# Overlapping two batch rows by two attention units, a tanh gate, and fewer TensorE passes in three small steps

## The reference

```
xn = layernorm(x)
# branch 1: attention with 16 heads of 8, causal
pressure = q k^T / sqrt(8), masked to -10000 above the diagonal
attn = 1 - tanh((pressure - threshold) / tau)^2, divided by its sum + 1e-6
s = (attn v) Wo^T
# branch 2: transformer block on xn
h = rmsnorm(xn); X = xn + softmax(q k^T / sqrt(8)) v wo      # not causal, 16 heads
h2 = rmsnorm(X); combine = weights of the 2 best of 8 experts, by token
moe = swiglu_shared(h2) + sum_e combine[e] * swiglu_e(h2)     # d_ff 256
g = silu(X + moe)
out = x + s * g
```

## Time and profile before

| what | value |
|---|---|
| median of three runs | 1170.88 us (1170.34 to 1171.27) |
| the profiled execution | 1171.43 us, span 1169.6 us |
| busy PE, DVE, ACT, POOL | 1055.8, 839.3, 648.9, 340.6 us |
| mean granted TensorE clock | 0.953 |
| from one gate to the next (first two) | 137.1 and 138.8 us |

### The profile page before, as it was taken

One profiled execution on the slowest core, in us unless ns is written; L12 is line 12 of the kernel. 1 busy time (PEld: TensorE's weight loads), 2 busy tenths in 40 slices (PEclk: granted clock), 3 DMA queues, 4 the chain that ended last, 5 costly groups with the idle time before them and its releaser, 6 DMA issues.

```text
span 1169.6 us, 18848 instructions
## 1 busy us (share of the span) xinstructions
PE 1055.8 (90%) x7112; PEld 487.0 (42%) x7112; DVE 839.3 (72%) x1692; ACT 648.9 (55%) x873; POOL 340.6 (29%) x178
## 2 busy tenths in 40 slices
PE   3469999899999899999999999989999999999998
PEld 1112465224651356424553246523464235532465
DVE  7366887659767687677876598765976868764872
ACT  4038842597227972388524983269722786248822
POOL 6500354005430335203351045301542033510023
PEclk9559999999998999999998999999999999989999
DMA  5530244104420045202350034400442012610020
GB/s 176 108 59 2 63 117 70 29 2 88 126 37 28 22 76 130 52 2 50 83 118 28 3 73 111 66 28 3 95 122 41 21 40 58 143 29 1 2 73 10
DMA packets 71787, 69.68 MB, mean 60 GB/s; under 512 B 8528, under 2 KB 63056, under 8 KB 71568
## 3 DMA queue, kind: packets, MB, share of 16 engines
q1 hardware_dynamic: 68928, 64.41, 25.0%
q10 hardware_dynamic: 2768, 4.06, 1.0%
HBM read 53.37 MB, written 14.81 MB: 58 GB/s over the span
## 4 chain that ended last, share of the span: by engine, by line
PE 66%; ACT 13%; DVE 12%; issue 4%; DMA 2%; SPq 2%; POOL 1%; ACTq 0%; POOLq 0%; DVEq 0%
PE O L977 12%; PE O L993 10%; ACT PT L534 7%; PE S L1009 6%; DVE PT L685 6%; PE M L919 6%; PE S L1011 6%; PE S L1010 6%; PE S L952 6%; PE M L916 5%; DVE nmax L648 3%; PE M L902 2%; ACT L534 2%; PE M L1082 2%; PE M L908 1%
## 5 line engine op out<-in xcount | busy, mean ns | idle before, releaser
L534 ACT ACTIVATE PT<-S 128x1024 f32<-128x1024 f32 (+1 forms) x448 | 420.0, 972 | 100.7 <-PE S L952 98.9
L648 DVE TENSOR_REDUCE nmax<-M 128x1 f32<-128x512 f32 x512 | 332.8, 685 | 121.1 <-PE M L916 75.5
L685 DVE SCALAR_TENSOR_TENSOR PT<-PT 128x768 f32<-128x768 f32 (+1 forms) x192 | 215.6, 1170 | 95.6 <-ACT PT L534 95.2
L977 PE MATMUL O<-PT,V 128*12 128x256 f32 (+3 forms) x2816 | 251.1, 438 | 0.0
L409 POOL TENSOR_TENSOR split<-split,parts 128x512 f32<-128x512 f32 x32 | 91.1, 2846 | 463.3 <-ACT parts L495 463.3
L952 PE MATMUL S<-stackQ,stackK 64*128 64x512 bf16 (+3 forms) x1024 | 202.1, 356 | 21.3 <-DMA stackQ<-mTZ 7.3
L568 ACT ACTIVATE PT<-S 128x1024 f32<-128x1024 f32 x72 | 73.9, 1027 | 257.9 <-PE S L1011 257.8
L424 POOL TENSOR_TENSOR PT<-PT,CB 128x1024 f32<-128x1024 f32 x56 | 133.3, 2387 | 283.7 <-DMA CB<-scrC 175.0
L1009 PE MATMUL S<-h2hi,wgu_hi 128*128 128x512 f32 x288 | 151.4, 526 | 0.0
L993 PE MATMUL O<-PT,wdn 128*128 128x512 f32 x288 | 142.8, 595 | 0.0
L916 PE MATMUL M<-KX,stackQ 128*128 128x512 bf16 x256 | 105.6, 414 | 26.0 <-DMA KX<-scrK 22.8
(11 more groups left out here) (177 smaller groups left out, 1034.8 us busy)
## 6 DMA issues: line engine op xcount, KB each, us to landing
CB<-scrC SPq DMA_DIRECT2D x64, 256.0 KB, 5.4
stackQ<-scrQ SPq DMA_DIRECT2D x192, 64.0 KB
stackK<-scrK SPq DMA_DIRECT2D x192, 64.0 KB
scrQ<-parts SPq DMA_DIRECT2D x16, 384.0 KB, 4.5
scrK<-parts SPq DMA_DIRECT2D x16, 384.0 KB, 8.7
KX<-scrK SPq DMA_DIRECT2D x96, 32.0 KB
PT<-in_w_gu ACTq DMA_DIRECT2D x2, 1152.0 KB, 7.8
xin<-in_x SPq DMA_DIRECT2D x8, 256.0 KB, 3.0
```

The costliest lines, as they stand in the source:

```text
L534: a.activation(PT[:, n % SLOTS, 2 * q * w:2 * q * w + 2 * w].rearrange("p (r n) -> p r n", r=2), S[k][:, :].rearrange("p (r n) -> p r n", ...
L648: v.tensor_reduce(nmax[:, h % 2, h // 2, t:t + 1], M[k][:, :], AX.X, ALU.max, negate=True).then_inc(m_read[k], 1)
L685: v.scalar_tensor_tensor(p, p, 1.0, p, ALU.subtract, ALU.mult).then_inc(weighed, 1)
L977: last = t_.matmul(O[k][32 * q:32 * q + VW, i0:i1], V[:, j, 4 * g + q, :], PT[:, n % SLOTS, w * q + at:w * q + at + i1 - i0], start=(j == ...
```

## The change

- **Rows overlap by two units.** The scores of units 0 and 1 of the next batch row, their exponentials, and the first maximum of run Y stand between the down products of experts 6, 7 and 8 of the present one. The gate goes into the next row: DVE takes part of it (`out_by_s`) in unit 0, ACT a tanh behind the exponentials of unit 1, DVE the rest (`out_gated`) in unit 1, and `outT` and its addition ride in unit 3. The store moves behind the load of `xin` on SP. Only the last row has its gate at its own end (`outL`).
- **The gate by tanh.** Silu(o) times s becomes (1 + tanh(o/2)) times (o times s/2): three operations instead of two.
- **Run X is cut in two**, X (pairs 0, 1) and W (pairs 2, 3), each with its own transpose, copy and four transfers. Unit 0 needs X alone, unit 4 needs W.
- **Fewer passes.** The masks of a unit with two key blocks are one matmul of 256 columns instead of two of 128. `suffix` uses sums of V that POOL makes (`VS`): 7 matmuls instead of 10. `combT` is a transpose instead of a product with the identity.

The core of the diff:

```diff
-RUNS = {"X": (0, 4), "Y": (4, 6), "Z": (6, 8)}
+RUNS = {"X": (0, 2), "W": (2, 4), "Y": (4, 6), "Z": (6, 8)}
...
-spread(MAX["Y"], {0: 1, 1: 4, 2: 4, 3: 4, 4: 3})
-spread(MAX["Z"], {4: 1, 5: 3, 6: 4, 7: 4, 8: 4})
+spread(MAX["Y"], {0: 1, 1: 3, 2: 4, 3: 4, 4: 4})
+spread(MAX["Z"], {5: 3, 6: 4, 7: 4, 8: 5})
+PLACES[3].insert(2, "outT")
...
-spread(MAX["X"], {EXPERT + e: n for e, n in enumerate((0, 0, 5, 4, 4, 5, 6, 6, 2))})
+spread(MAX["X"], {EXPERT + e: n for e, n in enumerate((0, 0, 5, 4, 4, 3))})
+spread(MAX["W"], {EXPERT + 5 + e: n for e, n in enumerate((2, 6, 6, 2))})
...
-PLACES[END - 1] += ["maxT_X"]
-PLACES[END] += ["outT"]
+PLACES[EXPERT + 6].insert(2, "maxT_X")
+PLACES[END] += ["maxT_W", "outL"]
...
+                g.tensor_tensor(VS[:, 1, :, :], V1[:, 2, :, 0:HD], V1[:, 3, :, 0:HD], ALU.add).then_inc(v_summed, 1)
+                wait_apart(pool, v_summed, it * 2 + 1)
+                g.tensor_tensor(VS[:, 0, :, :], V1[:, 1, :, 0:HD], VS[:, 1, :, :], ALU.add).then_inc(v_summed, 1)
...
-                act.wait_ge(down_done, it * DOWNS + DOWNS + DEPTH)
-                a.activation(gT[:, :], O[0][:, :], ACT.Silu).then_inc(o_read[0], 1)
+                if following:
+                    a.activation(warm[:, :], n1s[:, :], ACT.Exp)
+                    for q in range(2):
+                        weights(it + 1, 0, q)
+                    take(u, "maxT_W", bt)
+                    for q in range(2):
+                        weights(it + 1, 1, q)
+                act.wait_ge(out_scaled, it + 1)
+                a.activation(gT[:, :], O[0][:, :], ACT.Tanh, scale=0.5).then_inc(o_read[0], 1)
...
+            def out_by_s(it):
+
+                dve.wait_ge(down_done, (it + 1) * DOWNS + DEPTH)
+                dve.wait_ge(*read(ROWS[it], "proj1"))
+                v.tensor_tensor(sT[:, :], sT[:, :], O[0][:, :], ALU.mult).then_inc(out_scaled, 1)
+
+            def out_gated(it):
+
+                dve.wait_ge(o_read[0], (it + 1) * O_USES[0] + 1)
+                v.scalar_tensor_tensor(gT[:, :], gT[:, :], 1.0, sT[:, :], ALU.add, ALU.mult).then_inc(prod_ready, 1)
...
+                    if n == 0 and it > 0:
+                        out_by_s(it - 1)
+                    if n == 1 and it > 0:
+                        out_gated(it - 1)
...
+                        mask = never[:, :].unsqueeze(1).broadcast_to([128, len(js), 128])
...
-                        for j in range(t, NT):
-                            last = t_.matmul(M[k][:, t * 128:t * 128 + 128], (below if j == t else ones)[:, :],
-                                             V1[:, j, :, 0:HD], start=(j == t), stop=(j == NT - 1))
+                        last = t_.matmul(M[k][:, t * 128:t * 128 + 128], below[:, :], V1[:, t, :, 0:HD], start=True, stop=(t == NT - 1))
+                        if t < NT - 1:
+                            rest = V1[:, t + 1, :, 0:HD] if t == NT - 2 else VS[:, t, :, :]
+                            last = t_.matmul(M[k][:, t * 128:t * 128 + 128], ones[:, :], rest, start=False, stop=True)
...
-                        last = t_.matmul(M[k][0:E, t * 128:t * 128 + 128], comb[:, t, :], ident[:, :], start=True, stop=True)
+                        last = t_.transpose(M[k][0:E, t * 128:t * 128 + 128], comb[:, t, :], ident[:, :])
...
+                if following:
+                    first_scores(it + 1)
                 for _step in second_product(it, NE - 2):
                     pass
+                if following:
+                    work(u, it, "maxT_W")
+                    for q in range(2):
+                        scores(it + 1, 1, q)
+                    for name in ROWS[it + 1].places[0]:
+                        work(ROWS[it + 1], it + 1, name)
```

More of the change, by code:

```diff
@@ L119 @@
 FIRST = Uses(False, True)
-LOOP = Uses(True, True, FIRST.total)
-LAST = Uses(True, False, LOOP.row(B - 1).before)
+ROW0 = Uses(True, True, FIRST.total, behind=False)
+LOOP = Uses(True, True, tuple(f + r for f, r in zip(FIRST.total, ROW0.total)))
+ROWS = [ROW0] + [LOOP.row(it - 1) for it in range(1, B - 1)] + [Uses(True, False, LOOP.row(B - 2).before)]
 S_USES = UNITS + NE
@@ L369, in row @@
                     spread_weights(u, it)
-                wait_apart(sp, *read(u, "outT"))
-                sp.dma_start(out_t[bass.ds(it, 1)].rearrange("o p t d -> (o p) t d"), xres[:, :, :]).then_inc(written, 16)
-                wait_apart(sp, written, it * 16 + 16)
+                    store(u, it, "outL")
             sp.wait_ge(kset, 3)
             prepare(FIRST, 0)
-            for it in range(B - 1):
-                row(LOOP.row(it), it, True)
-            row(LAST, B - 1, False)
+            for it in range(B):
+                row(ROWS[it], it, it < B - 1)
         @block.gpsimd
@@ L601, in _ @@
             v = nc.vector
-            steps = [0, 0]
+            steps = [0]
             def step(ins, apart=False):
@@ L806, in row @@
                                 CB[:, E - 1, :].unsqueeze(1).broadcast_to([128, NFH, L]), ALU.mult).then_inc(routed_last, 1)
-                dve.wait_ge(o_read[0], it * O_USES[0] + O_USES[0] + 1)
-                dve.wait_ge(*read(u, "proj1"))
-                v.tensor_tensor(gT[:, :], gT[:, :], sT[:, :], ALU.mult).then_inc(prod_ready, 1)
-                k, _n = u("outT")
-                dve.wait_ge(*full(u, "outT"))
-                dve.wait_ge(xres_in, it * 16 + 16)
-                v.tensor_tensor(xres[:, :, :].rearrange("p t d -> p (t d)"), M[k][:, :],
-                                xres[:, :, :].rearrange("p t d -> p (t d)"), ALU.add).then_inc(m_read[k], 1)
-                assert steps[0] <= DVE_ROW and (not following or steps[0] == DVE_ROW), steps
+                if not following:
+                    out_by_s(it)
+                    out_gated(it)
+                    take(u, it + 1, "outL")
             for k in range(2):
@@ L1158, in _ @@
             first_scores(0)
-            for it in range(B - 1):
-                row(LOOP.row(it), it, True)
-            row(LAST, B - 1, False)
+            for q in range(2):
+                scores(0, 1, q)
+            for name in ROWS[0].places[0]:
+                work(ROWS[0], 0, name)
+            for it in range(B):
+                row(ROWS[it], it, it < B - 1)
 _INS = ["x", "par", "n1w", "n2w", "w1", "w2", "router", "w_gu", "w_dn"]
```

124 lines of the change are left out of this document (71 added, 53 removed).

## The result

| | median | runs |
|---|---|---|
| before | 1170.61 us | 4 (1169.96 to 1171.27) |
| after | 1155.16 us | 4 (1154.38 to 1157.05) |

The ratio is 0.988 [0.986, 0.990]: the change gains 15 us where 39 were forecast. 1155 lies outside the range of 1121 to 1152. The profiled execution took 1157.05 us with a span of 1155.2, the slowest of the four.

What follows compares the result with a forecast made beforehand. PE was taken to bound the experts, with PE, ACT and DVE waiting in turn at row ends. Terms -26.6 - 9.6 - 0.8 - 3.3 + 0.7 + 0.8 = -38.8 us from 1171.4 gave 1132; range 1121 to 1152.

Steps and rivals of the forecast that it cites:

- What bounds the kernel, and D to Z: Experts bound by PE; from D, a row's last down product, to run Z's split 23.8 us instead of 27.8.
- rivals (a) to (d): Behind D: clock still falls 1144 (0.18); DVE keeps waits 1149 (0.14); DVE back-to-back 1117 (0.10); no boundary gain 1160 (0.05).
- The rule of the Trainium skill on transposes and the clock gate: Transposes don't count as busy for the clock, so outT's four in unit 3 could help bring on a fall: 1144.
- One sign of being wrong: Listed signs: PE waits in the tail for S1 or W's split, at outT, or longer for Z's rows at unit 12.
- the prediction's 0.25: Behind D, each us at half clock was priced at 0.25 us of added time.
- A boundary gains 3.8 us: At each batch row's end the overlap saves 3.8 us; seven boundaries give -26.6 us.
- D at 349.3: 0.2 us later: Row's tail on PE: 7.6 us from 341.7, so the last down product ends its wait 0.2 us later, without new waits.
- Run X in two: in the shade of the experts' PE work but for the transpose, +0.7: In the experts: one more transpose and DVE split per row, hidden but for the transpose; +0.7 us in all.
- First row: -3.3: Kernel start: unit 0's wait for transfers hidden under W's maxima, 4.2 us less 0.9 for a second run.
- Suffix, combT, masks: Fewer PE passes: suffix and combT 1.2 us per row, -9.6 for eight; masks 0.1 per row, -0.8.
- The last gate: End of the last row: three gate operations in a chain instead of two, +0.8 us.
- the five rivals: Four alternatives behind D, and a fifth: clock falls ahead of D in the experts, slower than before, 1184, chance 0.03.

Runs made afterwards that it cites:

- e5: The changed kernel with a Silu in place of the gate's tanh, so the output is wrong and two table loads return per boundary: 1155.72 us, ratio 0.985.
- e7: The changed kernel with only unit 0 of the next row overlapped; unit 1's scores behind the last down product, its exponentials behind the tanh: 1156.52 us, ratio 0.987.
- b1: The kernel before with only the fewer passes (masks, suffix, combT); no row overlap, Silu gate, run X whole: 1160.93 us, ratio 0.991.
- e2: The changed kernel with the split of run X moved ahead of expert 6's product and its transpose one expert later: 1149.06 us, ratio 0.981.
- e3: The changed kernel with POOL beginning its weight of expert 5 only when the split of run X is done: 1150.99 us, ratio 0.981.
- c2: The changed kernel with Q1/K1 loads behind X and W at the start, X's split later, W's maxima counts 2, 6, 5, 3: 1141.11 us, ratio 0.975.
- c3: The changed kernel with Q1/K1 loads behind X and W at the start, POOL waiting for X's split, W's counts 2, 5, 6, 3: 1143.14 us, ratio 0.975.
- e6: The changed kernel with X and W as one run of four pairs, as before; rows still overlap: 1189.72 us, ratio 1.014.
- e1: The changed kernel with the first row's Q1 and K1 loads issued on SP behind the transfers of X and W: 1150.76 us, ratio 0.982.
- e4: The changed kernel with Q1/K1 loads behind X and W at the start, and two first-row maxima of Y ahead of unit 1's scores: 1153.19 us, ratio 0.984.
- c1: The changed kernel with Q1/K1 loads behind X and W at the start, X's split later, W's maxima counts 3, 6, 5, 2: 1148.02 us, ratio 0.979.

## Why the prediction was wrong, step by step

**What bounds the kernel, and D to Z: right.** The split of Z is 23.8 us behind D, as worked out, and the clock doesn't fall there; rivals (a) to (d) did not come. The rule of the Trainium skill on transposes and the clock gate ("TensorE: Matmul & The Clock Gate", Part 4) decided nothing here: `outT`'s transposes ride in unit 3 and the granted clock stays at 1.00 around them in all seven boundaries. e5 and e7 show in addition that DVE's queue paces this stretch: neither two table loads nor a unit's exponentials put back behind D move it by more than 0.5 us. So the gain here did not come from the table loads that the tanh saves, and only in small part from unit 1. One sign of being wrong came in part: at unit 12 PE waits for Z's rows for 1.79 us in one row of the change and 1.22 in another, where it is 0.9 in the rest and 0.9 to 1.0 before. b1, with before's order, has it too (1.90 and 2.06 us), so it comes without the overlap too; the period with the 1.79 is 136.2 us long.

How much of the stretch's gain is the clock's and how much the new order's can be read from b1. Its first boundary has before's order and no fall. These are the 29 us from its D, and the split of Z that follows:

```profile
214.72:243.72 29.00, 25.80 (x212) 6.21 (x212) 24.37 (x55) 24.32 (x27) 2.37 (x3) 1.00 0.10 29
```

```profile
240.42 0.17 DVE L666 CAST mhZ<-nmax 128x16 bf16<-128x16 f32 x1
```

That is 25.7 us from D to Z. The seven of before have a mean of 27.8, the change has 23.8: some 2.1 us are the clock's and 1.9 the order's. It is one boundary. It also prices the clock higher than the prediction's 0.25 where little of it is lost: the boundaries of 0.94 take 27.0 us in before and in b1, 1.3 more for 3.5 us at half clock.

**"A boundary gains 3.8 us": the D of this term failed.** "D at 349.3: 0.2 us later" was the tail of the row. In the frame from the start of expert 6's down product it forecast 7.4 us to D; it was 7.2 before (341.91 to 349.06) and it is 8.3. PE waits nowhere in it (the addition of x1 at 350.56 and the last down product at 351.56 are shown above):

```profile
345.17 1.88 PE L1035 MATMUL O<-PT,wdn 128*128 128x512 f32 x4
...
346.89 0.38 PE L960 MATMUL M<-KX,stackQ 128*128 128x512 bf16 x1
...
347.20 0.61 PE L994 MATMUL S<-stackQ,stackK 64*128 64x512 bf16 x4
...
347.74 1.99 PE L1035 MATMUL O<-PT,wdn 128*128 128x512 f32 x4
...
349.65 0.23 PE L969 MATMUL M<-identb,mhW 128*32 128x128 bf16 x1
349.81 0.60 PE L994 MATMUL S<-stackQ,stackK 64*128 64x512 bf16 x4
350.25 0.38 PE L963 MATMUL M<-stackK,stackQ 48*128 48x512 bf16 x1
```

From start to start: down products 1.72 + 1.91 + 1.88 = 5.5 (taken at 5.2), two maxima 0.31 each = 0.62 (0.45), scores 0.54 + 0.44 = 0.98 (0.88), x1 1.00 (0.89), the transpose 0.16 (0.20): 8.3 for 7.6. The mechanism was right and its sizes were off by 0.65 us; another 0.2 was a slip of the frame, since 341.7 was taken for the start of a down product that began at 341.91. No wait for S1 or for W's split came. Seven tails lose 0.9 each against the forecast, 6 us. This account is read from rows; no experiment isolates it.

**"Run X in two: in the shade of the experts' PE work but for the transpose, +0.7": wrong, the largest step in the rows.** It cost 1.6 us a row between experts 3 and 5, less the 0.2 that come back before expert 6: 1.35 us a row, some 8 in six periods, where 0.1 was charged. e2, e3, c2 and c3 show two causes. The cast of the split lay beside POOL's product and took 1.39 us, with PE's transpose behind it, and the words of X and W crowd one stage (seven in six steps). With both mended c2 and c3 take 17.3 and 17.2 us from expert 3 to expert 6, the change 18.4, before 17.1. The prediction had looked at the number of DVE's operations and not at what runs on POOL beside them. The other side of the same step was left out too: the cut is what makes the overlap pay. Without it (e6) the kernel is slower than before by 14 parts in 1000; the change is faster by 12.

**"First row: -3.3": wrong in sign, the largest single step.** +5.5 us at the first split of Z and +6.3 at the first x1 in this pair of traces; by the means of the traces of each order +3.1, so that part of the size is chance and the sign rests on few executions. That the waits for X's rows grew is what the program and e1 show. "The scores waited for transfers, and now those of X are under the maxima of W" took the transfers as if they stood alone. For the end of a row the prediction had looked at what stands ahead on each queue, and here it had not: at the start the 24 loads of `Q1` and `K1` are issued on SP before them. e1 shows 4 to 8 us of it (5.0 on the mean of five traces against five); with e1, e2 and the counts (c2) the first x1 comes at 206.4 us, where the forecast's terms give 204.9.

**Suffix, combT, masks: right.** -10.4 forecast, -9.4 measured (b1), and 1.3 us a row in the stretch where they lie, in b1 and in the change (84.5 to 85.0 us for 85.9 to 86.2, without the rows in which unit 12 waited longer). In the chain the suffix is seven pieces of two passes, 0.22 us each, and `combT` is one piece (`PE M L1133 x4`) of 0.44 us. **The last gate: right.** +1.0 for +0.8 from the last x1 to the end. The last row gained 7.0 instead of 5.3: it has neither the words of the next row nor the overlap, and so neither loss. In before it had a clock of 0.94 from 1100 to 1130 us, some 3.5 us at half clock, which no term took up.

Added up by stretches: the start 11 of the 24 us (0.8 of it the first tail), experts 3 to 6 with the split of X 7.5, the tails of the six periods 5, and 3 for what the six periods gain less than forecast up to expert 3, part of it the later rows of Z; the last row is 2 the other way.

**The range.** Of the five rivals four stood behind D, and none was an error of the start or of the cut of run X, whose two terms were carried as single values. A lower bound of nothing gained for the first row (3.3 us more) would alone have moved the upper end from 1152 to 1155.3. That would have covered the number and still not the cause.

## What to carry to other kernels

A small step that is put "in the shade" needs the row of every engine beside it: a 0.17 us cast became 1.39 us because POOL's product ran in the same microsecond, and PE stood behind it. The first rows of X came as late as the 24 loads ahead of them, so at the start of a kernel list what the same queue issued before a small transfer. When a gain is forecast at a boundary, measure whole periods from one mark to the next, split by marks inside; most of this loss lay outside the stretch that was argued over. And take a start that runs only once from several traces: here the same start differed by 5 us between executions.

## What the hardware showed that was not expected

- A cast of 128x16 elements from float32 to bf16 in SBUF takes 0.17 us on DVE alone, and 1.39 us when it is issued in the middle of POOL's 2.4 us product of 128x1024; it ends 0.03 us behind that product. DVE's maxima from PSUM beside the same product take their usual 0.64 each. The subtraction behind the cast (0.18) starts when POOL is done, so it tells nothing.
- Four transfers of a few KB, issued at 59.28 us behind 24 of 64 KB on the same queue, landed at 76.2 in this execution; with the same order the scores that wait for them began between 72.3 (e7) and 78.4 us (e3), and behind the other order between 68.8 and 70.2 (e1, e4, c1, c2, c3).
- A wait of PE for Z's rows of 1.55 to 1.95 us at unit 12 was followed by a granted clock of 0.75 to 0.78 over some 7 us in rows of e1, c1, e3 and c3, and by 1.00 in the change (1.79 us), e2 (1.62) and b1 (1.90 and 2.06).
- The clock fell in the middle of a row's end once PE stood for 4 us ahead of a down product (e6), and didn't fall at all where PE had work in the same place (the change).
